# Clamped turned scores, softmax sums as rows of the value product, and a split down product

## The reference

```python
# L0 attention: 8 batches of 512 tokens, 256 wide, 16 heads of 16
q = concat(q_sem, rope(q_geo)); k = concat(k_sem, rope(k_geo))
scores = einsum('bhqd,bhkd->bhqk', q, k) * 16 ** -0.5
scores = where(causal, scores, float32_min)
out = einsum('bhqk,bhkd->bhqd', softmax(scores), v)
y = out.reshape(B, S, 256) @ Wo.T
# L1 ffn: 8 experts with inner width 176, two of them for a token
h = silu(x @ w1_gate) * (x @ w1_up) * routing_weight
y = h @ w2
```

## Time and profile before

| | |
|---|---|
| median of 3 runs | 6342.38 us (6337.89 to 6351.53) |
| profiled execution | 6344.69 us, span 6342.9 us |
| PE busy | 5705.4 us, 90% |
| DVE, ACT, POOL busy | 4353.2, 3415.3, 3607.3 us |
| attention, 60 to 860 us | PE 680.46, DVE 330.31, ACT 207.27, POOL 109.38 us busy |
| experts, 5925 to 6343 us | PE 412.70, DVE 131.53, ACT 52.18 us busy |

### The profile page before, as it was taken

How to read it: one execution, slowest core, us unless ns; L and a number is a source line. 1 busy time by engine, 2 the same in 40 slices (tenths; PEclk the granted TensorE clock), 3 DMA queues, 4 the chain that set the end, 5 groups by cost and what they waited for, 6 DMA issues and landing times. The chain is left out here.

```text
span 6342.9 us, 129354 instructions
## 1 busy us (share of the span) xinstructions
PE 5705.4 (90%) x41980; PEld 4051.0 (64%) x41980; DVE 4353.2 (69%) x6508; ACT 3415.3 (54%) x4604; POOL 3607.3 (57%) x4085
## 2 busy tenths in 40 slices
PE   5899858836999999999999999999999999974699
PEld 3444437724777777777777777777777777763587
DVE  4444445554888888888888888888888888835233
ACT  2222222223777777777777777777777777731111
POOL 1111100003888888888888888888888888820000
PEclk8899879968999999999999999999999999986899
DMA  3333310013111111111111111111111111121100
GB/s 90 82 82 77 85 64 17 26 60 100 29 30 28 33 28 30 28 33 28 30 28 33 28 30 28 33 28 30 28 33 28 30 28 33 28 87 60 41 23 20
DMA packets 428606, 263.11 MB, mean 41 GB/s; under 512 B 264741, under 2 KB 359525, under 8 KB 427653
## 3 DMA queue, kind: packets, MB, share of 16 engines
q1 hardware_dynamic: 420100, 253.98, 15.5%
q10 hardware_dynamic: 8448, 8.39, 0.4%
HBM read 186.73 MB, written 66.85 MB: 40 GB/s over the span
## 5 line engine op out<-in xcount | busy, mean ns | idle before, releaser
L1516 ACT ACTIVATE ss_r<-ss_pssum,ss_eps 128x512 f32<-128x512 f32 x512 | 352.9, 689 | 900.4 <-PE ss_pssum L1447 900.4
L1576 DVE SCALAR_TENSOR_TENSOR ss_psb<-ss_psb,ss_norm,ss_r 128x512 f32<-128x512 f32 x512 | 362.8, 754 | 446.1 <-ACT ss_r L1518 446.1
L1447 PE MATMUL ss_pssum<-ss_sq,ss_pairssum 128*128 128x512 f32 x1024 | 570.9, 639 | 56.9 <-DVE ss_fr L1564 56.9
L1328 POOL TENSOR_TENSOR ss_sq<-ss_sq 128x512 f32<-128x512 f32 x256 | 329.6, 1287 | 453.0 <-ACT ss_sq L1525 453.0
L48 PE MATMUL ss_psb<-x_hi,ss_whi 128*128 x1024 | 529.5, 517 | 4.4 <-DVE ss_fr L1564 4.4
L1428 PE MATMUL ss_psse<-ss_rot 64*128 64x128 f32 x8224 | 530.0, 279 | 0.8 <-POOL ss_rot L1310 0.8
L1358 POOL TENSOR_TENSOR ss_own<-ident,ss_tk 128x512 f32<-128x512 f32 x512 | 524.5, 1046 | 0.0
L1428 PEld LDWEIGHTS ss_psse<-ss_rot 64*128 64x128 f32 x8224 | 480.6, 188 | 44.1 <-issue 43.0
L48 PE MATMUL ss_psc<-x_hi,ss_whi 128*128 x1024 | 505.0, 493 | 0.0
L566 DVE TENSOR_REDUCE a_top<-a_pss 128x2 f32<-128x256 f32 (+3 forms) x256 | 204.5, 820 | 346.0 <-PE a_pss L377 346.0
L50 PE MATMUL ss_psb<-x_hi,ss_wlo 128*128 x1024 | 404.0, 395 | 0.0
(11 more groups left out here) (346 smaller groups left out, 15558.8 us busy)
## 6 DMA issues: line engine op xcount, KB each, us to landing
ss_dtb<-time_steps SPq DMA_DIRECT2D x516, 128.0 KB, 2.8
ss_wraw<-in_w_state SPq DMA_DIRECT2D x264, 80.0 KB, 2.3
head_rows<-a_yhi SPq DMA_DIRECT2D x64, 256.0 KB, 6.0
a_qs<-head_rows SPq DMA_DIRECT2D x32, 384.0 KB, 5.6
a_ks<-head_rows SPq DMA_DIRECT2D x32, 384.0 KB, 5.7
ss_xp<-x_heads SPq DMA_DIRECT2D x33, 256.0 KB, 4.2
y_heads<-ss_yo SPq DMA_DIRECT2D x132, 64.0 KB, 2.4
head_rows<-a_ylo SPq DMA_DIRECT2D x32, 256.0 KB, 6.4
```

The costliest lines, as they stand in the source:

```text
L1328: G.tensor_tensor(sq[:, 0, 0], sq[:, 0, 0], sq[:, 0, 1], ALU.add).then_inc(ss_b, 1)
L1447: M(p_sum[:], pairs_sum[:], sq[:, q, 0], start=True, stop=True).then_inc((sum_b, sum_c)[q], 1)
L1516: A(r[:, q], p_sum[:], ACT.Ln, scale=1.0 / N1, bias=eps[:, 0:1]).then_inc(ln, 1)
L1576: link.mark(S(bank[:, e, :], bank[:, e, :], norm[:, 2 * q + e:2 * q + e + 1], r[:, q], ALU.mult, ALU.mult))
```

## The change

Four things change in the attention. The turned scores are no longer masked on TensorE (`plain_block`); VectorE clamps each diagonal block with a minimum (`keep_past`, `limit` is -3e38 where masked and 3e38 elsewhere), and the exponential waits for that. The unused half of each strip of `v_pad` holds ones, so the sums come out as 16 rows beside the values; there are two output banks, one for each quad, and no product with `ones`. ScalarE copies the bank (`take`), SyncE moves the rows of sums onto the partitions of the values (`gather_sums`, 4 DMAs of 16 rows a quad), and VectorE divides at t = 1 in place of t = 0, with `own`, a column that is one on a quad's own rows. And in SyncE's list `maxima_in` stands ahead of `spread_rows`. In the experts, h and the down weights are split into rounded halves and the down product is made of three single-pass products.

```diff
-        p_o, p_sum = ps("o", [P, SEQ]), ps("sum", [P, SEQ])
+        p_o = [ps(f"o{q}", [P, SEQ]) for q in range(2)]
...
+            def gather_sums(half, quad):
+                sp.wait_ge(o_copied, half * 2 + quad + 1)
+                for c in range(4):
+                    to, at = 32 * c + DH * quad, 32 * c + DH * (1 - quad)
+                    sp.dma_start(sums[to:to + DH, :], o_sb[at:at + DH, quad, :]).then_inc(sums_in, 16)
+
             def step(b, f, t, n):
                 half = 2 * n + f
                 after = (b, 1) if f == 0 else (b + 1, 0)
                 if is_pair(4 * half + t + 1):
                     maxima_out(b, 4 * f + t + 1)
-                if t == 0 and is_half(half + 1):
-                    stack(*after, 0)
+                if t < 2 and is_half(half + 1):
+                    stack(*after, t)
+                if is_pair(4 * half + t + 1):
+                    maxima_in(b, 4 * f + t + 1)
                 if t == 0 and is_half(half + 1):
                     spread_rows(*after, 1)
-                if t == 1 and is_half(half + 1):
-                    stack(*after, 1)
                 if t == 2 and is_half(half + 2):
                     spread_rows(b + 1, f, 0)
-                if is_pair(4 * half + t + 1):
-                    maxima_in(b, 4 * f + t + 1)
+                if t == 3 and is_half(half):
+                    gather_sums(b * 2 + f, 0)
+                if t == 0 and is_half(half - 1):
+                    gather_sums(b * 2 + f - 1, 1)
...
-            G.memset(v_pad[:], 0.0).then_inc(cleared, 1)
+            G.memset(v_pad[:], 1.0).then_inc(cleared, 1)
...
+            def plain_block(bank, pieces):
+                for at, width, left, right in pieces:
+                    for e in range(2):
+                        last = M(bank[:, e, at:at + width], left(e), right(e), start=True, stop=True)
...
-                block_of(p_st, 1, pieces).then_inc(st_done, 1)
+                plain_block(p_st, pieces).then_inc(st_done, 1)
...
-                    for psum, left in ((p_o, lambda c: v_pad[:, kt, f, quad, c, :]), (p_sum, lambda c: ones[:, quad, :])):
-                        for c in range(4):
-                            last = M(psum[32 * c:32 * c + 32, kt * P:SEQ], left(c), pt[:, c // 2, c % 2, at:at + width],
-                                     start=quad == 0 and j == 0, stop=quad == 1 and j == 2, skip_group_check=True)
+                    for c in range(4):
+                        last = M(p_o[quad][32 * c:32 * c + 32, kt * P:SEQ], v_pad[:, kt, f, quad, c, :], pt[:, c // 2, c % 2, at:at + width],
+                                 start=j == 0, stop=j == 2, skip_group_check=True)
...
-                act.wait_ge(st_done, (b * 8 + 4 * f + t) * FILLS + j + 1)
+                act.wait_ge(keep_done, (b * 8 + 4 * f + t) * FILLS + j + 1)
...
+            def take(half, quad):
+                act.wait_ge(pv_done, (half * 2 + quad + 1) * FILLS)
+                at_least(act, ot_done, half)
+                A(o_sb[:, quad], p_o[quad][:], ACT.Copy).then_inc(o_copied, 1)
...
+                if t == 2 and here:
+                    take(b * 2 + f, 0)
+                if t == 0 and is_half(half - 1):
+                    take(b * 2 + f - 1, 1)
...
+            V.tensor_scalar(limit[:], above_f[:, 1, :], 1.5e38, 2.0, ALU.add, ALU.mult).then_inc(t_loaded, 1)
+            for q in range(2):
+                V.tensor_reduce(strips[:, q], g.ident[:].rearrange("p (c w) -> p c w", w=2 * DH)[:, :, DH * q:DH * (q + 1)], AX.X, ALU.add).then_inc(t_loaded, 1)
+            dve.wait_ge(t_loaded, 52)
+            for q in range(2):
+                last = V.tensor_reduce(own[:, q:q + 1], strips[:, q], AX.X, ALU.add)
+            last.then_inc(t_loaded, 1)
...
+            def keep_past(b, f, t, j):
+                dve.wait_ge(st_done, (b * 8 + 4 * f + t) * FILLS + j + 1)
+                for at in ((0,), (0, 3 * P), (0,))[j]:
+                    edge = p_st[:, :, at:at + P]
+                    last = V.tensor_tensor(edge, edge, limit[:].rearrange("p (o w) -> p o w", o=1).broadcast_to([P, 2, P]), ALU.min)
+                last.then_inc(keep_done, 1)
...
+                if here:
+                    keep_past(b, f, t, 0)
                 if ahead:
                     maximum(b, f, t, 0)
                 if is_pair(4 * half + t + 1):
                     turn_maxima(b, 4 * f + t + 1)
                 if t == 3 and outs:
                     add_residual(b, 1)
+                if here:
+                    keep_past(b, f, t, 1)
                 if t % 2 and is_half(half + 2):
                     turn(b + 1, f, t // 2, 0)
                 if ahead:
                     maximum(b, f, t, 1)
                 if t % 2 and is_half(half + 2):
                     turn(b + 1, f, t // 2, 1)
-                if t == 0 and is_half(half - 1):
-                    dve.wait_ge(pv_done, (b * 2 + f) * 2 * FILLS)
-                    V.reciprocal(rec[:, 0:SEQ // 2], p_sum[:, 0:SEQ // 2])
+                if t == 1 and is_half(half - 1):
+                    dve.wait_ge(sums_in, (b * 2 + f) * 128)
+                    V.reciprocal(rec[:, 0:SEQ // 2], sums[:, 0:SEQ // 2])
+                if here:
+                    keep_past(b, f, t, 2)
                 if t == 2 and outs:
                     add_residual(b, 0)
                 if ahead:
                     maximum(b, f, t, 2)
-                if t == 0 and is_half(half - 1):
-                    V.reciprocal(rec[:, SEQ // 2:SEQ], p_sum[:, SEQ // 2:SEQ]).then_inc(rec_done, 1)
+                if t == 1 and is_half(half - 1):
+                    V.reciprocal(rec[:, SEQ // 2:SEQ], sums[:, SEQ // 2:SEQ]).then_inc(rec_done, 1)
                     at_least(dve, wo_done, b * 2 if f else b * 2 - 2)
                     dve.wait_ge(rec_done, b * 2 + f)
-                    V.tensor_tensor(ot[:, 1 - f, :], p_o[:], rec[:], ALU.mult).then_inc(ot_done, 1)
+                    for q in range(2):
+                        V.scalar_tensor_tensor(o_sb[:, q], o_sb[:, q], own[:, q:q + 1], rec[:], ALU.mult, ALU.mult).then_inc(part_done, 1)
+                    dve.wait_ge(part_done, (b * 2 + f) * 2)
+                    V.tensor_tensor(ot[:, 1 - f, :], o_sb[:, 0], o_sb[:, 1], ALU.add).then_inc(ot_done, 1)
...
             def down(b, q, s):
-                pe.wait_ge(h_done, b * ET + s + 3)
+                pe.wait_ge(high_done, b * ET + s + 1)
                 for n in range(TPB):
-
-                    last = nc.tensor.matmul(pd[:, n, :], h[:, q % 2, n * P:(n + 1) * P], wd[:, s, :],
-                                            start=s == 0 and n % 2 == 0, stop=s == ET - 1 and n % 2 == 1,
-                                            skip_group_check=True)
+                    rows = h_hi[:, q % 2, n * P:(n + 1) * P]
+                    nc.tensor.matmul(pd[:, n, :], rows, wd_hi[:, s, :], start=s == 0 and n % 2 == 0, stop=False,
+                                     skip_group_check=True)
+                    nc.tensor.matmul(pd[:, n, :], rows, wd_lo[:, s, :], start=False, stop=False, skip_group_check=True)
+                pe.wait_ge(low_done, b * ET + s + 1)
+                for n in range(TPB):
+                    last = nc.tensor.matmul(pd[:, n, :], h_lo[:, q % 2, n * P:(n + 1) * P], wd_hi[:, s, :],
+                                            start=False, stop=s == ET - 1 and n % 2 == 1, skip_group_check=True)
                 last.then_inc(down_step, 1)
...
+                    act.wait_ge(h_done, n + 3)
+                    act.wait_ge(down_step, n + 1)
+                    nc.scalar.activation(h_hi[:, q % 2], h[:, q % 2], ACT.Copy).then_inc(high_done, 1)
...
+            V.tensor_copy(wd_hi[:], wd[:]).then_inc(d_split, 1)
+            dve.wait_ge(d_split, 1)
+            V.tensor_tensor(wd_lo[:], wd[:], wd_hi[:].bitcast(FP32), ALU.subtract).then_inc(d_split, 1)
...
-                    dve.wait_ge(down_step, n + 1)
                     V.tensor_tensor(h[:, q % 2], pb[q % 2][:], silu[:, q % 2], ALU.mult).then_inc(h_done, 1)
+                    dve.wait_ge(high_done, n + 1)
+                    V.tensor_tensor(h_lo[:, q % 2], h[:, q % 2], h_hi[:, q % 2].bitcast(FP32), ALU.subtract).then_inc(low_done, 1)
```

More of the change, by code:

```diff
@@ L178, in causal_attention @@
     s_done, max_done, mhi_done, mlo_done = sem("s"), sem("max"), sem("mhi"), sem("mlo")
+    keep_done, o_copied, sums_in, part_done = sem("keep"), sem("ocopied"), sem("sumsin"), sem("part")
     st_done, exp_done, pv_done, rec_done, ot_done = sem("st"), sem("exp"), sem("pv"), sem("rec"), sem("ot")
@@ L193, in causal_attention @@
         tables = sb("tables", [P, 4, SEQ])
-        above_f, above = sb("abovef", [P, 2, P]), sb("above", [P, 2, P], BF16)
+        above_f, above = sb("abovef", [P, 2, P]), sb("above", [P, P], BF16)
+        limit = sb("limit", [P, P])
         t1, t2, y = sb("t1", [P, SEQ]), sb("t2", [P, SEQ]), sb("y", [P, SEQ])
@@ L201, in causal_attention @@
```

(30 more changed lines are left out.)

6 lines of the change are left out of this document (4 added, 2 removed).

## The result

The changed kernel takes 6327.82 us, median of 16 runs (6318.55 to 6332.09), beside 6343.09 us of the kernel before, measured with it: the ratio is 0.9974, 95% interval 0.9966 to 0.9981. That is 15 us faster where 46 were forecast. The profiled execution's span is 6326.3 us against 6342.9.

What follows compares the result with a forecast made beforehand. Attention was bound by TensorE in steps 1 and 3, by the maxima loop through DRAM in 0 and 2; experts by TensorE. 6344.7 less 30 (attention) and 16 (experts) gave 6298.7, as median 6296 us; range 6235 to 6362.

Steps and rivals of the forecast that it cites:

- Experts: Experts' phase: twelve single-pass products replace the down product, 22 us less 5 at batch ends, rounded to 16 us gained.
- SyncE's order: Attention step 0: maxima reads before spread writes, 8.0 us from turn to next start; step becomes 10.8 us (was 13.0).
- Clamps: Attention, between turned scores and exponential: four VectorE clamps of 256 elements, 0.43 us each, 1.7 us a step.
- VectorE's queue: Attention step 1: VectorE's queue ends at 13.6 us and delays step 2's turn; steps 1 and 2 take 21.4 us together.
- the floor of 6.0: Attention loop: 6.03 us from a turn to the next step's start where no large transfer is ahead.
- The clock: Attention steps 1 and 2: waits halve TensorE's clock, costing 2 us a half, 32 us in all; bounds nothing and 7.6.
- rival C: Attention: half clock from the wait ahead of step 1 into step 3, 6 us a half, 6360 us, slower; chance 0.20.
- point of decision: Attention: from 4.9 us a half on, the half clock has eaten all that the loop and the experts gave.
- A: The forecast itself: attention gains 30 us, experts 16, time 6275 to 6320, steady clock 0.80 or more; chance 0.42.
- the sign of being wrong: Attention: the prediction is wrong if steps 1 and 2 together are over 24 us.
- its end: Attention's end: the last half's sums need copy, issues, landing and two passes, and draining steps expose clamps: 8 us once.
- The relief of TensorE: Attention: sums and mask products go, 8.3 us a half, 133 us over 16 halves if TensorE alone set the pace.

Runs made afterwards that it cites:

- Both fillers: The changed kernel with unread TensorE products of 512 columns added in both waits, 11 at the end of step 0 and 10 at the end of step 1: 0.9899.

## Why the prediction was right or wrong

**Experts: right.** The product of 256 columns takes 0.120 us (0.122 taken), twelve 1.44 us (1.46). The step fell by 0.29 us (0.25), and the batch-end wait is 4.6 us in eight (5). "The new split of the weights lies beside the weight DMAs" was wrong by a small term: VectorE's two passes end beside GpSimd's first pass, which took 5.39 us instead of 3.15, and the first product comes 1.9 us later in the phase. The phase gained 17.0 us (16).

**SyncE's order: right.** From the turn at 386.79 to the next start at 394.82 is 8.03 us (8.0), step 0 takes 10.82 (10.8). The four gather issues took SyncE 2.46 us (1.7 taken), in a gap of its queue. That the order alone is worth 55 us was not worked out apart from the rest, and so it was not seen that the other parts of the attention would have to take that away.

**Clamps: right in size** (0.43 us for one, 0.76 for two back to back; 0.43 each taken).

**VectorE's queue: right as a sum.** Taken: 21.4 us for steps 1 and 2. With TensorE at the full clock they take 20.2. In the change the first clamp of step 2 comes 14.6 us after step 1's start (13.6) and the turn at 16.1 (15.4); the 1.87 us that VectorE is idle ahead of its second clamp were not in the sum. In that time TensorE's projection products of 512 columns, one at 397.58 and the next at 398.01, start 0.43 us apart instead of 0.23. From that turn to step 3 it is 7.77 us instead of the floor of 6.0, because TensorE's own work of step 2, the output product of 3.24 us in it, ran at half clock and ended last.

**The clock: this is the step that failed.** "I take 2 us, since one of the two waits is near the one that was paid for before and what it cost is already in the 46.3". The half without any cost of the clock was forecast as 41.6 us, and it is 46.04: 4.4 us. The runs give its parts. Both fillers bring the half to 518.81 / 12 = 43.2, 2.8 us less. What is left, 1.6 us, lies in step 3, which there takes 10.8 us on the mean in first halves (10.0 forecast) and 11.4 in second halves (8.8). The first 0.8 us, 0.4 for each half, are not the clock's, since it is 1.00 in that step, in the change too; the second-half step that was read took 11.79 us at a clock of 0.60. So the clock cost about 4 us a half, an estimate from these numbers, and was priced at 2.

The mechanism, its place and its sign were those of rival C, whose price was 6 and whose point of decision 4.9 us a half; the size lies between the forecast and C, as does the clock of the six batches, 0.76 where A wanted 0.80 or more and C under 0.7. Steps 1 and 2 took 24.1 us on the mean of the 12 halves, just over the 24 that the forecast had named as the sign of being wrong. 2.4 us more in these 12 halves are 29 us, nearly all of the 32 by which the time was missed. Outside them the attention came out even: its start gained 7.1 us (the first half of all, whose step 1 has no division to do, took 42.4 us after 49.2), and its end lost 7.3 (8 taken). By the Trainium skill ("TensorE: Matmul & The Clock Gate", section "HAM oscillation — how this bites in real kernels") waits that come again and again put the array back to half clock each time. The trace agrees with that rule: in the change waits of 3.44 and 2.02 us in one half were both followed by half clock. The forecast cited it and then priced it at half of what it cost. The second wait was the mistake: a new wait of 2 us behind step 1 is not a lesser copy of the one before it; here it had a slow stretch of its own behind it.

**The relief of TensorE: the error behind it.** The forecast said that 133 us would follow if TensorE alone set the pace, and that it doesn't. It still saw the removed products as a gain where they end last, in steps 1 and 3. What showed is that with the removed work the clock at which the rest runs fell too: busy time fell by 38.9 us in six batches where 8.3 x 12 = 100 us of work had gone at the full clock.

**Small slips in the sums.** The eight passes of the old down product at (1.89 - 0.38) / 7 us are 1.73 us, not 1.71. The gain was counted in 15 halves and the clock's cost in 16, which is 2 us. Neither changes the outcome.

**Open.** How the 58 us of the sums part divide between queue and clock can't be said, since each makes the other. What share the gathers have, up to 12 us, is not settled. Why the clock falls in step 3 of second halves with both waits filled was not tried; in the step ahead of the one read, TensorE waits 1.38 and 0.78 us for exponentials and 0.40 us for maxima, and no filler stood in these waits.

## What to carry to other kernels

Before work is taken from an engine, ask what ends last in each step there: relief that turns into waiting gains nothing, and on TensorE it can lower the clock of what remains, so price every new wait of 2 us as a slow stretch of its own. That is the upper price: in the run with two fillers, four waits of 1.4 to 2.0 us had none behind them. Change the order of a DMA queue first and alone, small transfers that a loop waits for ahead of large ones that it doesn't: here those moved lines alone gave 0.9%, and the rest of the rewrite hid most of it. A change of several parts should be costed and run part by part, since one part may pay for the loss of another.

## What the runs showed of the hardware

- A wait of 2.02 us was followed by 10.2 us at half clock, one of 1.91 us by 23.9 us, with no idle time of TensorE in the longer stretch.
- Filling one wait moved the slow stretch to the next wait in the second halves of the batches. Filling both raised the granted clock from 0.76 to 0.91 and cut 48 us, with 21 useless products of 512 columns a half.
- GpSimd's fp32 pass took 5.39 us when it started 0.71 us into VectorE's pass of 3.09 us, and 3.15 us without it. It ended 3.0 us after VectorE's pass did, as if it had run only then. The run with the split alone shows the same, 5.41 us.
- A single-pass product of 256 columns with a new weight load each time started every 0.120 us at full clock: the load was hidden.
